# Biases added to the residual's tokens by GpSimd; the norms' scaling on ScalarE with shifts from GpSimd

## Time and profile before

| | us |
|---|---|
| median of 3 runs | 2510.22 (2498.77 to 2511.85) |
| the profiled execution's own time | 2505.16 |
| its span, first to last instruction | 2503.3 |
| TensorE busy (86% of the span) | 2163.3 |
| VectorE busy (64%) | 1595.5 |
| ScalarE busy (55%) | 1368.4 |
| GpSimd busy (38%) | 943.7 |

### The profile page before, as it was taken

One profiled execution on the slowest core, in us unless ns is written; L12 is line 12 of the kernel. 1 busy time (PEld: TensorE's weight loads), 2 busy tenths in 40 slices (PEclk: granted clock), 3 DMA queues, 4 the chain that ended last, 5 costly groups with the idle time before them and its releaser, 6 DMA issues.

```text
span 2503.3 us, 93142 instructions
## 1 busy us (share of the span) xinstructions
PE 2163.3 (86%) x39704; PEld 1734.1 (69%) x39704; DVE 1595.5 (64%) x5098; ACT 1368.4 (55%) x2531; POOL 943.7 (38%) x1080
## 2 busy tenths in 40 slices
PE   6997889998899979999799997999889998898860
PEld 4775777776677757777577776777667776676730
DVE  4886766776566756677466665676656764555535
ACT  3664555665466645666356654566555554554535
POOL 3443443443344433444334433444334443333300
PEclk9999999999899989999899998999999999999985
DMA  6775655655456645555355554555455553434429
GB/s 173 210 201 157 189 154 150 167 168 149 117 163 170 169 119 153 167 166 159 98 165 155 163 158 124 166 168 155 137 142 162 167 146 107 132 117 116 138 78 394
DMA packets 335102, 393.57 MB, mean 157 GB/s; under 512 B 40033, under 2 KB 239458, under 8 KB 334690
## 3 DMA queue, kind: packets, MB, share of 16 engines
q1 hardware_dynamic: 333842, 386.62, 53.0%
q10 hardware_dynamic: 848, 0.99, 0.1%
HBM read 208.29 MB, written 160.27 MB: 147 GB/s over the span
## 4 chain that ended last, share of the span: by engine, by line
PE 59%; DVE 29%; ACT 5%; issue 4%; DMA 1%; POOL 1%; SPq 0%; POOLq 0%; DVEq 0%; ACTq 0%
PE ps_hid L714 9%; PE ps_y L725 9%; PE ps_proj L577 6%; PE ps_o L662 6%; DVE onorm L951 5%; PE ps_s L643 4%; PE ps_hid L744 3%; PE ps_s L649 3%; PE ps_t L675 3%; DVE negmax L939 3%; DVE xn L993 3%; PE ps_max L633 3%; PE ps_y L694 2%; PE ps_y L681 2%; DVE stats L980 2%
## 5 line engine op out<-in xcount | busy, mean ns | idle before, releaser
L1097 POOL TENSOR_TENSOR prob_lo<-prob,prob_hi 128x512 f16<-128x512 f32 x528 | 611.0, 1157 | 915.1 <-ACT prob_hi L812 915.1
L811 ACT ACTIVATE prob<-ps_s 128x512 f32<-128x512 f32 x528 | 313.8, 594 | 401.2 <-PE ps_s L649 395.7
L946 DVE RECIPROCAL rden<-ps_o 128x8 f32<-128x8 f32 x528 | 107.4, 203 | 523.6 <-PE ps_o L662 522.4
L939 DVE TENSOR_REDUCE negmax<-ps_max 128x8 bf16<-128x512 f32 x528 | 360.5, 683 | 118.1 <-PE ps_max L633 113.7
L951 DVE TENSOR_TENSOR onorm<-ps_o,rden 64x128 f32<-64x128 f32 x1056 | 304.5, 288 | 25.6
L812 ACT ACTIVATE prob_hi<-ps_s 128x512 f16<-128x512 f32 x528 | 313.2, 593 | 0.0
L662 PE MATMUL ps_o<-vb,prob_hi 128*128 128x68 f16 x4224 | 294.7, 197 | 3.0 <-DVE onorm L951 2.9
L725 PEld LDWEIGHTS ps_y<-w_sb,hid 128*128 128x128 f32 x2048 | 266.8, 196 | 31.7 <-issue 26.8
L714 PE MATMUL ps_hid<-xf,w_sb 128*128 128x512 f32 x512 | 286.1, 641 | 3.0 <-ACT yconv L869 2.1
L725 PE MATMUL ps_y<-w_sb,hid 128*128 128x128 f32 x2048 | 277.8, 280 | 0.6 <-ACT hid L850 0.6
L662 PEld LDWEIGHTS ps_o<-vb,prob_hi 128*128 128x128 f16 x4224 | 261.6, 100 | 9.6 <-issue 5.3
(11 more groups left out here) (116 smaller groups left out, 3557.9 us busy)
## 6 DMA issues: line engine op xcount, KB each, us to landing
k_rows<-k_flat SPq DMA_DIRECT2D x256, 256.0 KB, 3.2
qs<-q_rows SPq DMA_DIRECT2D x512, 128.0 KB, 3.2
ks<-k_rows SPq DMA_DIRECT2D x128, 512.0 KB, 4.7
q_rows<-q_flat SPq DMA_DIRECT2D x128, 256.0 KB, 2.4
vb<-v_flat SPq DMA_DIRECT2D x128, 136.0 KB, 4.2
vb<-values_out SPq DMA_DIRECT2D x128, 136.0 KB, 2.9
xin<-in_x SPq DMA_DIRECT2D x64, 256.0 KB, 3.1
self_out<-xa SPq DMA_DIRECT2D x64, 256.0 KB, 3.4
```

Of the source, the lines that this page charges most:

```text
L811: activation(prob[:, pair_no(u, k) % 2, :], ps_s[:, :], ACT.Exp)
L939: v.tensor_reduce(negmax[:, pair_no(u, k) % 2, :], ps_max[:, :].rearrange("p (a t) -> p a t", t=TOK), AX.X, ALU.max, negate=True).then_inc ...
L1097: g.tensor_tensor(prob_lo[:, i, :], prob[:, i, :], prob_hi[:, i, :], ALU.subtract).then_inc(s_prob, 1)
```

## The change

- The matmul with the bias row is gone, and with it `ones2`, `brow`, its preparation on VectorE and the nine DMAs of SyncE for it. GpSimd adds the biases to the tokens instead, in two new stages. `bias` adds in place to the unit's tokens in `xin` or `xlow`, after the last projection has read them; `bias2` writes `xf + b2` to a new buffer `xf_plus`. The residual's transposes wait for these.
- `apply` and `apply2` move from VectorE to ScalarE with their due times unchanged: `Identity(scale * x + bias)`, where scale is the root and bias is `-mean * root`, both one value to a partition.
- GpSimd makes that bias: a `tensor_scalar` (mean times -1) beside the eps, and a `tensor_tensor` (times the root) behind the power. Line 1088 and line 1091 stay.
- The biases come in three more columns of `columns_sb`.

```diff
-            project=6.2, stats=6.5, rstd=6.55, apply=6.9, spread=7.56, spread_out=7.66, store=8.0, pool=8.6)
+            project=6.2, stats=6.5, rstd=6.55, apply=6.9, spread=7.56, spread_out=7.66, store=8.0, pool=8.6, bias=-4.7)
-             spread_out=7.36, h0=8.2, relu0=8.4, h1=9.2, relu1=9.4, resid2=9.45, f0=9.47, h2=10.2, relu2=10.4,
+             spread_out=7.36, bias=-4.6, bias2=7.75, h0=8.2, relu0=8.4, h1=9.2, relu1=9.4, resid2=9.45, f0=9.47, h2=10.2, relu2=10.4,
-           rstd=3.45, apply=3.8, spread=4.68, spread_out=4.76, pad=5.2, expand=5.7, kk0=6.85, kk0_hi=7.05,
+           rstd=3.45, apply=3.8, spread=4.68, spread_out=4.76, bias=-5.5, pad=5.2, expand=5.7, kk0=6.85, kk0_hi=7.05,
...
-            sp.dma_start(brow_f[:, :], bias_rows).then_inc(s_bias, 16)
...
-            def setup_bias():
-                sp.wait_ge(s_prep_v, 3)
-                for part, src in ((0, brow_hi), (1, brow_lo)):
-                    for p in range(PAIRS):
-                        sp.dma_start(brow[part:part + 1, :, p, :], src[:, :].rearrange("p (a c) -> p a c", a=3)
-                                     ).then_inc(s_brow, 16)
...
-            def residual(ps, pairs, src, bias):
+            def residual(ps, pairs, src):
                 for p in range(pairs):
-                    mm(ps[:, C * p:C * p + C], src[:, C * p:C * p + C], ident[:, :], is_transpose=True,
-                       start=(p == 0), stop=False, skip_group_check=True)
-                return mm(ps[:, 0:C * pairs], ones2[:, :], brow[:, bias, 0:pairs, :].rearrange("p a c -> p (a c)"),
-                          start=False, stop=False, skip_group_check=True)
+                    done = mm(ps[:, C * p:C * p + C], src[:, C * p:C * p + C], ident[:, :], is_transpose=True,
+                              start=(p == 0), stop=False, skip_group_check=True)
+                return done
...
-                residual(ps_y, u.pairs, tokens_of(u), which(u)).then_inc(s_resid, 1)
+                pe.wait_ge(s_plus, plus_no["bias", u.seq, None])
+                residual(ps_y, u.pairs, tokens_of(u)).then_inc(s_resid, 1)
...
-                residual(ps_y2, PAIRS, xf[:, u.no % 2, :], 2)
+                pe.wait_ge(s_plus2, u.no + 1)
+                residual(ps_y2, PAIRS, xf_plus).then_inc(s_resid2, 1)
...
+            def apply_to(u):
+                if before_spread[u.seq] is not None:
+                    act.wait_ge(s_t, turn_no["spread", before_spread[u.seq].seq, None])
+                act.wait_ge(s_rstd, y_no["project", u.seq, None])
+                for p in range(u.pairs):
+                    activation(xn[:, C * p:C * p + C], ps_y[:, C * p:C * p + C], ACT.Identity, bias=shift1[:, p:p + 1],
+                               scale=rstd[:, p:p + 1]).then_inc(s_xn, 1)
+
+            def apply2_to(u):
+                if u.no:
+                    act.wait_ge(s_t, out_turn[u.no - 1])
+                act.wait_ge(s_rstd2, u.no + 1)
+                for p in range(PAIRS):
+                    activation(xn2[:, C * p:C * p + C], ps_y2[:, C * p:C * p + C], ACT.Identity, bias=shift2[:, p:p + 1],
+                               scale=rstd2[:, p:p + 1]).then_inc(s_xn2, 1)
...
-                for p in range(u.pairs):
-                    v.tensor_scalar(xn[:, C * p:C * p + C], ps_y[:, C * p:C * p + C], mv[:, p, 0:1],
-                                    rstd[:, p:p + 1], ALU.subtract, ALU.mult).then_inc(s_xn, 1)
...
+            def root_and_shift(var, var_eps, to, neg_mean, to_shift, pairs, count, mv_done, var_done, root_done, rstd_done):
                 pool.wait_ge(mv_done, count)
-                g.tensor_tensor(var_eps[:, 0:pairs], var[:, 0:pairs, 1], eps[:, 0:pairs], ALU.add
-                                ).then_inc(var_done, 1)
+                g.tensor_tensor(var_eps[:, 0:pairs], var[:, 0:pairs, 1], eps[:, 0:pairs], ALU.add)
+                g.tensor_scalar(neg_mean[:, 0:pairs], var[:, 0:pairs, 0], -1.0, None, ALU.mult).then_inc(var_done, 1)
                 pool.wait_ge(var_done, count)
                 g.tensor_tensor(to[:, 0:pairs], var_eps[:, 0:pairs], half_neg[:, 0:pairs], ALU.pow
+                                ).then_inc(root_done, 1)
+                pool.wait_ge(root_done, count)
+                g.tensor_tensor(to_shift[:, 0:pairs], neg_mean[:, 0:pairs], to[:, 0:pairs], ALU.mult
                                 ).then_inc(rstd_done, 1)
+
+            def add_bias(u):
+                pool.wait_ge(s_proj, proj_no["q" if u.kind == "cross" else "v", u.seq, None])
+                t, m = tokens_of(u), which(u)
+                g.tensor_scalar(t, t, add_sb[:, m:m + 1], None, ALU.add).then_inc(s_plus, 1)
+
+            def add_bias2(u):
+                pool.wait_ge(s_t_taken, turn_no["spread", u.seq, None])
+                if u.no:
+                    pool.wait_ge(s_resid2, u.no)
+                g.tensor_scalar(xf_plus[:, :], xf[:, u.no % 2, :], add_sb[:, 2:3], None, ALU.add).then_inc(s_plus2, 1)
```

More of the change, by code:

```diff
@@ L112, in stages_in_order, with attention_conv @@
     return [r[1:] for r in row]
-def attention_conv(nc, x, wq, wk, wv, wf, bias_rows, columns, w1, w2, convw, consts, out):
+def attention_conv(nc, x, wq, wk, wv, wf, columns, w1, w2, convw, consts, out):
     units = units_in_order()
@@ L161, in attention_conv @@
     resid_no = numbered("resid")
+    plus_no = numbered("bias")
     same_b = {}
@@ L256, in attention_conv @@
         xn = sb("xn", [128, SW])
+        neg_mean = sb("neg_mean", [128, PAIRS])
+        shift1 = sb("shift1", [128, PAIRS])
+        neg_mean2 = sb("neg_mean2", [128, PAIRS])
+        shift2 = sb("shift2", [128, PAIRS])
         stats2 = sb("stats2", [128, PAIRS, 6])
@@ L340, in attention_conv @@
         s_on = sem("s_on")
+        s_plus = sem("s_plus")
+        s_plus2 = sem("s_plus2")
         s_resid = sem("s_resid")
+        s_resid2 = sem("s_resid2")
         s_y = sem("s_y")
@@ L878, in _ @@
                        ).then_inc(s_prep_a, 1)
-            act.wait_ge(s_prep_v, 4)
+            act.wait_ge(s_prep_v, 1)
             act.wait_ge(s_prep_g, 2)
             act.wait_ge(s_prep_a, 1)
-            walk({"q_hi": q_hi, "k_hi": k_hi, "v_hi": v_hi, "exp": exponentials, "turned": take_turned,
+            walk({"q_hi": q_hi, "apply": apply_to, "apply2": apply2_to, "k_hi": k_hi, "v_hi": v_hi, "exp": exponentials, "turned": take_turned,
                   "spread_out": take_spread, "relu0": lambda u: take_hidden(u, 0),
@@ L967, in stats_of @@
                 done.then_inc(s_mv, 1)
-            def apply_to(u):
-                if before_spread[u.seq] is not None:
-                    dve.wait_ge(s_t, turn_no["spread", before_spread[u.seq].seq, None])
-                dve.wait_ge(s_rstd, y_no["project", u.seq, None])
-                for p in range(u.pairs):
-                    v.tensor_scalar(xn[:, C * p:C * p + C], ps_y[:, C * p:C * p + C], mv[:, p, 0:1],
-                                    rstd[:, p:p + 1], ALU.subtract, ALU.mult).then_inc(s_xn, 1)
             def stats2_of(u):
@@ L986, in stats2_of @@
                 done.then_inc(s_mv2, 1)
-            def apply2_to(u):
-                if u.no:
-                    dve.wait_ge(s_t, out_turn[u.no - 1])
-                dve.wait_ge(s_rstd2, u.no + 1)
-                for p in range(PAIRS):
-                    v.tensor_scalar(xn2[:, C * p:C * p + C], ps_y2[:, C * p:C * p + C], mv2[:, p, 0:1],
-                                    rstd2[:, p:p + 1], ALU.subtract, ALU.mult).then_inc(s_xn2, 1)
             def pool(u):
@@ L1099, in rstd_of @@
             def rstd_of(u):
-                inv_sqrt(mv, vareps, rstd, u.pairs, y_no["project", u.seq, None], s_mv, s_var, s_rstd)
+                root_and_shift(mv, vareps, rstd, neg_mean, shift1, u.pairs, y_no["project", u.seq, None], s_mv, s_var,
+                               s_root, s_rstd)
             def rstd2_of(u):
-                inv_sqrt(mv2, vareps2, rstd2, PAIRS, u.no + 1, s_mv2, s_var2, s_rstd2)
+                root_and_shift(mv2, vareps2, rstd2, neg_mean2, shift2, PAIRS, u.no + 1, s_mv2, s_var2, s_root2, s_rstd2)
             def expand(u):
@@ L1146, in _ @@
             walk({"prob_lo": split_prob, "rstd": rstd_of, "rstd2": rstd2_of, "expand": expand, "k_wrap": wrap_keys,
-                  "k_take": take_keys})
+                  "k_take": take_keys, "bias": add_bias, "bias2": add_bias2})
             pool.wait_ge(s_bn, 1)
```

34 lines of the change are left out of this document (10 added, 24 removed).

## The result

| | before | after |
|---|---|---|
| median, us | 2511.03 (2498.77 to 2517.35, 4 runs) | 2582.59 (2582.02 to 2605.57, 4 runs) |
| span of the profiled execution, us | 2503.3 | 2580.4 |
| mean granted clock of TensorE | 0.945 | 0.946 |

The changed kernel is slower: ratio 1.0313, interval 1.0244 to 1.0382. The forecast was 2580 in 2490 to 2650.

A forecast was written before the change was run, and what follows sets the result against it. The bound was taken to change hands within each 32.4 us period: VectorE in a 13.63 us stretch, TensorE nearly throughout the rest. Terms 58 + 13 + 4 + 1.5 - 1.7 = +75 on 2505.2 gave 2580 us, range 2490 to 2650.

The forecast's parts named there:

- Part 1: Bias matmuls removed from TensorE: -0.43 us a period, in the part that TensorE bounds.
- Part 2: Shift made on GpSimd: negated mean and product lengthen each norm's chain by 0.37 us, bounds 0.25 to 0.56.
- Part 3: Scaling on ScalarE: 458 ns each, four in 1.54 us; ScalarE has room, so order matters, not load.
- Stalls B and C: Scaling ahead of `exp` on ScalarE: cross unit's (B) +0.85 us at its stretch's end, self unit's (C) +1.2 us.
- VectorE's relief: Rival: freeing VectorE in its tight stretch wins, if ScalarE's queue adds nothing: 2423 us, chance 0.14.
- Stall A: `apply2` on ScalarE ahead of `k_hi`: `out` on TensorE ends 0.54 us later, `v` starts 0.33 later.
- The period: One period of the mixed self and cross units: 0.85 - 0.43 + 1.2 = +1.6 us; 36 periods give +58.
- Part 4: Units standing alone: self-only +1.1 us each, +13; cross-only +4; last three norms +1.5.
- the second rival: Stalls lower TensorE's clock, slower still: +82 us, 2662, chance 0.12; self-only units among those hit.
- Part 5: Kernel start: tokens' load no longer behind nine bias DMAs; first projection waits for GpSimd's last memset: -1.7 us.
- Part 6: 200 bias adds on GpSimd, at most 1157 ns each, hidden by slack: 0 us; without slack up to +232.
- The clock rival: Gaps from the stalls drop TensorE's clock to 1.2 GHz 48 more times: +82 us, 2662, chance 0.12.

The follow-up runs named there:

- e1: Changed kernel with both scalings back on VectorE and the plain root chain; biases still added by GpSimd: 2481.01 us, ratio 0.9898 to the kernel before.
- e6: Changed kernel with only `apply2` on ScalarE, placed behind `k_hi`; `apply` back on VectorE with the plain root chain: 2524.06 us, ratio 1.0086.
- e11: e1 with its VectorE scalings fed by GpSimd's root and shift, the longer chain: 2577.37 us, ratio 1.0285 to the kernel before.
- e3: Changed kernel with the three bias additions and TensorE's waits for them left out: 2593.52 us, ratio 1.0342 to the kernel before.
- e4: Changed kernel with the self units' `apply` moved behind `exp` (6.9 to 7.03), low units' `resid` 3.0 to 3.1: 2536.63 us, ratio 1.0133.
- e12: e11 with `out` moved from 13.8 to 14.15 and `out_take` from 13.9 to 14.3: 2583.35 us, ratio 1.0308 to the kernel before.
- e9: Changed kernel, scalings still on ScalarE, with self `apply` behind `exp`, `apply2` behind `k_hi`, `out` and `out_take` later, low `resid` 3.1: 2518.16 us, ratio 1.0050.
- e2: Kernel before, bias matmul kept, with only the scalings moved to ScalarE and fed by GpSimd's shifts: 2620.13 us, ratio 1.0454.
- e5: Changed kernel with `apply2` moved behind `k_hi` on ScalarE (due 13.4 to 13.45): 2584.99 us, ratio 1.0326 to the kernel before.
- e13: e12 with VectorE's self-unit `k_lo` moved ahead of the scaling (-6.45 to -6.61): 2511.06 us, ratio 1.0007 to the kernel before.
- e10: e1 with `out` moved from 13.8 to 14.15 and `out_take` from 13.9 to 14.3: 2495.62 us, ratio 0.9954 to the kernel before.

## Why the prediction was right, point by point

The time came out within 3 us of the forecast, and that is partly luck: the self-only and cross-only parts brought 23 us more than forecast and the mixed part 18 less.

- **Part 1** held: -0.39 us a period for -0.43 (e1). The half by itself gained 1.0%, or 26 us; the prediction had 15 over 36 periods, 3 to 6 in the cross-only units and 1.7 at the start.
- **Part 2**: +0.49 us on the chain for +0.37, inside 0.25 to 0.56. The negated mean is overlapped by a third only: `rstd` starts 0.47 us after the chain does, where it was 0.28, so it costs 0.19 of the 0.28 that it would cost in full.
- **Part 3, the scaling**: 458 ns as taken, four in 1.50 us for 1.54. The Trainium skill's rule ("ScalarE: Activation LUTs", section "What ACT_TABLE_LOAD costs") gives an estimate of 479 ns; the measurement is 21 ns below it and decides.
- **Stalls B and C** came where they were put: the scores of 4.0 and 8.0 waited for `prob_hi`, and behind the latter the transposes for `spread_out`. Their idle times were 0.76 (B) and 0.65 + 0.39 us (C). VectorE's relief was of no use: in a period it is busy 19.13 of 34.12 us and stands before `k_lo` for 1.76 us until ScalarE's `k_hi` is done.
- **Stall A** was undersized in its main row: TensorE stands 1.33 us ahead of `out`, where before it stood 0.79. That is the +0.54 which the prediction named and then dropped from the period's sum, since the stretch was VectorE's. By the sum this was harmless: A's 0.54 and B's 0.76, less the 0.26 and 0.25 ahead of `v` and `turn` that are gone, make +0.79 where +0.85 was forecast for the stretch. e6 and e11 show that this gap matters.
- **The period**: +1.75 for +1.6. But it holds only in regular periods, and these are 28 and not 36. In five of them the kernel before had a low clock itself (34.0 us), and the difference is 0.1; the ten periods beside low units are 0.2 to 2.3 us shorter, 10 in all, where the forecast had 0. The mixed part brought +40 for the forecast's +58: the term that was too large.
- **Part 4**: the term that was too small. The self-only units brought +29 (from -2.3 to +27.1) for +13. Their stall was as forecast, 14.04 us for 12.79, +1.25; but nine took 15.0 to 16.0, with the granted clock at 0.91 from 40 to 250 us where it had been 0.98. There the second rival came true. The cross-only part and tail brought +12 for +5.5.
- **Part 5** held: the first projection starts at 13.10, released by GpSimd's last memset. By the first norm the lead is 3.6 us, twice the 1.7.
- **Part 6**: the result held (e3), its bound failed. 1157 ns was called the upper end, from a row with two tensors; the add took 1575. TensorE waited 1.5 us in all for `prob_lo` in the mixed part, so the slack covered it.
- **The clock rival** was judged by the mean clock, and that stayed at 0.946. It was true in the self-only part and latent in the rest: taking a stall out (e4), leaving only `apply2` on ScalarE (e6) or only lengthening the chain (e11) lets the clock fall in 22, 20 and 28 of the 28 regular periods, and in e11 this costs about what the stalls did. The prediction went by gaps of 0.25 us and said that the trace before neither shows nor excludes the rule; it overlooked the 0.79 us ahead of `out`, behind which five regular periods of the kernel before ran at a clock of 0.95. The rule of the Trainium skill that was cited for it ("TensorE: Matmul & The Clock Gate", section "A second HAM failure mode: psum-queue depth-cycling", short idle times between groups of matmuls can make the clock swing) agrees with e4, e6, e11 and e12; by it alone the changed kernel's regular periods, with more such gaps and a clock of 1.00, should have been hit as well, and they were not.

Which of two prices is paid is thus open to small things, but both come from one cause: the scaling is ready later, and TensorE waits for it or for work that stands behind it. With the order mended the changed form costs 0.5% (e9) instead of 3.1%, and e1 is the fastest version that was run: the biases on GpSimd, the scaling on VectorE, 1.0% faster than before.

What stays open: what decides behind which gap the clock falls. All of the kernels below have about 1.3 us of idle time ahead of `out`; of the 28 regular periods of the profiled execution, these ran at a lower clock:

| | stall C in place | periods at a lower clock |
|---|---|---|
| changed kernel | yes | 0 |
| e3 | yes | 2 |
| e2 | yes | 6 |
| e5 | yes | 8 |
| e6 | no | 20 |
| e4 | no | 22 |
| e11 | no | 28 |

e4 differs from the changed kernel by stall C's order alone (and `resid` of the low units), so taking that stall out is what let the clock fall there; why, no run shows. The order in the period doesn't settle it by itself, since in e6 periods of the same order and the same gap go both ways; when the gap comes may count, and no run varied that. Nor is the changed kernel safe from it: one of its four executions took 2605.57 us at a mean clock of 0.931, of which there is no trace.

## What to carry to other kernels

- Before an operation moves to an engine with room, write down what stands behind it in that engine's order and when it was ready. A load of 63% (ScalarE's, after the change) says nothing; a wait for a third engine ahead of urgent work that is ready does.
- Split a loss into TensorE's busy and idle time. If the same matmuls have become longer and the granted clock is lower, the loss is the clock's, and here the order of the work around the gap cured it; check where the gap went, since moving one product may open it elsewhere (e12, e13).
- Take a change of two halves apart early: here one half was worth 1.0% and the other cost 4.5%.
- Count in how many periods the clock was low before reading a single one: the same kernel shows both kinds (e6, e10, and the kernel before).
